# Gates of an adaLN block computed as columns, the last chunk's second half done block by block, and a new order of the stages

## The reference

```python
mod = (_silu(L0_c) @ L0_wmod).reshape(L0_c.shape[0], 6, 1, -1)
sa, ca, ga, sb, cb, gb = (mod[:, 0], mod[:, 1], mod[:, 2], mod[:, 3], mod[:, 4], mod[:, 5])
ga = (2 * (ga >= 0) - 1) * jnp.maximum(jnp.abs(ga), 0.25)
gb = (2 * (gb >= 0) - 1) * jnp.maximum(jnp.abs(gb), 0.25)
h = _layernorm(x, axis=-1) * (1 + ca) + sa
x = x + ga * attn(h)
h = _layernorm(x, axis=-1) * (1 + cb) + sb
x = x + gb * ffn(h)
```

## Time and profile before

| | |
|---|---|
| median of 3 runs | 470.56 us (470.47 to 470.79) |
| the profiled execution | 470.41 us |
| its span | 468.4 us |
| busy: PE, DVE, ACT, POOL | 420.9, 356.3, 302.0, 268.8 us |
| mean granted clock of PE | 0.984 |

### The profile page before, as it was taken

One profiled execution on the slowest core, in us unless ns is written; L12 is line 12 of the kernel. 1 busy time (PEld: TensorE's weight loads), 2 busy tenths in 40 slices (PEclk: granted clock), 3 DMA queues, 4 the chain that ended last, 5 costly groups with the idle time before them and its releaser, 6 DMA issues.

```text
span 468.4 us, 11145 instructions
## 1 busy us (share of the span) xinstructions
PE 420.9 (90%) x4170; PEld 270.2 (58%) x4170; DVE 356.3 (76%) x675; ACT 302.0 (64%) x974; POOL 268.8 (57%) x309
## 2 busy tenths in 40 slices
PE   3589949989989999999999999999897979888976
PEld 0265527666677656776667766666474744453432
DVE  4769989897978889878878786768867896646531
ACT  2445567987888798688568867666876866522210
POOL 4220726311775677756448776667528779976271
PEclk9799979999999999999999999999999999999999
DMA  8999763352474669536738836556842264672532
GB/s 318 235 397 388 207 206 46 59 123 47 80 147 113 158 133 202 143 84 115 181 72 157 163 49 145 111 139 117 156 115 46 47 136 90 153 142 45 136 80 77
DMA packets 144901, 65.09 MB, mean 139 GB/s; under 512 B 134704, under 2 KB 134960, under 8 KB 144464
## 3 DMA queue, kind: packets, MB, share of 16 engines
q1 hardware_dynamic: 144704, 64.37, 57.7%
q10 hardware_dynamic: 144, 0.02, 0.1%
HBM read 26.63 MB, written 4.19 MB: 66 GB/s over the span
## 4 chain that ended last, share of the span: by engine, by line
PE 51%; DVE 16%; POOL 10%; DMA 9%; ACT 6%; issue 5%; SPq 2%; ACTq 0%; POOLq 0%; DVEq 0%
PE F L1024 15%; PE C L1133 12%; PE C L1024 10%; PE W L1024 3%; PE S L1179 3%; PE W L1196 3%; ACT prob L705 3%; DMA xa<-in_x_dram 3%; POOL prob L584 2%; DVE p L915 2%; DMA gT<-g 2%; PE S L1024 2%; DMA xb<-in_x_dram 2%; DVE nm L909 2%; DVE qk L895 2%
## 5 line engine op out<-in xcount | busy, mean ns | idle before, releaser
L1133 PE MATMUL C<-hT,cw 128*128 128x256 f16 x864 | 108.4, 277 | 13.0 <-DVE cv L886 6.9
L584 POOL TENSOR_TENSOR prob<-prob,rinv 128x1024 f32<-128x1024 f32 x32 | 62.4, 1948 | 73.7 <-DVE rinv L920 73.7
L1133 PEld LDWEIGHTS C<-hT,cw 128*128 128x128 f16 x864 | 83.0, 99 | 32.1 <-issue 7.4
L705 ACT ACTIVATE prob<-S,nms 128x128 f32<-128x128 f32 x256 | 89.9, 377 | 7.1 <-DVE p L915 6.0
L1024 PE MATMUL F<-btw,gT 128*128 128x512 f16 x336 | 74.8, 379 | 2.2 <-DMA gT<-g 2.1
L676 ACT ACTIVATE qk<-C,bqk 128x256 f16<-128x256 f32 x128 | 52.6, 479 | 14.2 <-PE C L1024 13.4
L895 DVE SCALAR_TENSOR_TENSOR qk<-C,bqk,qk 128x256 f16<-128x256 f32 x128 | 54.3, 474 | 4.6 <-ACT qk L676 4.6
L1024 PEld LDWEIGHTS F<-btw,gT 128*128 128x128 f16 x336 | 32.5, 98 | 40.7 <-DMA gT<-g 2.9
L705 ACT ACTIVATION_READ_ACCUMULATOR prob<-S,nms 128x1 f32 x256 | 55.5, 217 | 0.0
L1024 PE MATMUL C<-cv,pw 128*128 128x256 f16 x384 | 50.4, 273 | 2.4 <-DVE cv L886 1.9
L915 DVE SCALAR_TENSOR_TENSOR p<-prob,p 128x1024 f16<-128x1024 f32 x32 | 48.3, 1509 | 4.6 <-ACT p L714 4.3
(11 more groups left out here) (187 smaller groups left out, 722.2 us busy)
## 6 DMA issues: line engine op xcount, KB each, us to landing
xa<-in_x_dram SPq DMA_DIRECT2D x10, 512.0 KB, 4.3
xb<-in_x_dram SPq DMA_DIRECT2D x6, 512.0 KB, 5.0
wmb<-in_wmod_dram SPq DMA_DIRECT2D x1, 3072.0 KB, 19.1
out_dram<-xb SPq DMA_DIRECT2D x12, 256.0 KB, 2.4
cw_raw<-in_cw_dram SPq DMA_DIRECT2D x3, 768.0 KB, 5.3
raw<-in_cw_dram SPq DMA_DIRECT2D x3, 768.0 KB, 5.2
wma<-in_wmod_dram SPq DMA_DIRECT2D x4, 512.0 KB, 6.9
bt_raw<-in_btw_dram SPq DMA_DIRECT2D x2, 1024.0 KB, 9.7
```

Source lines behind the costliest of these rows:

```text
L584: nc.gpsimd.tensor_tensor(prob[:], prob[:], rinv[:, i % 2].unsqueeze(2).broadcast_to([P, 8, P]), ALU.mult).then_inc(p_normal, 1)
L705: ins = nc.scalar.activation(prob[:, h], S[i % len(S)][h // 4][:, (h % 4) * P:(h % 4 + 1) * P], ACT.Exp, bias=nms[:, i % 2, h:h + 1], scal ...
L1133: ins = nc.tensor.matmul(bank_c[:, 0:CH], cw[:, i, a, c, tap, :], hT[:, j % 2, b, c, OWN - 1 + tap:OWN - 1 + tap + CH], start=step == 0, s ...
```

## The change

Four things are changed.

1. **Gates as columns.** row:0:2 makes one group of rows in place of two copies. A new stage cols:0:2 turns it into columns, cols:0:1 does so with gb as well, and `clamp` works on 128 x 8 values, in five operations (a copy comes first). Each pick is four products of 128 columns with a full identity in place of one of 512. The tile sel is now a view of that identity, so POOL makes two fewer constants.
2. **First stages by hand.** cols:0:0 comes before hs:1:0; hs:1 is two stages, a block each; all of the first 33 convolution products stand together; pj's last operation on DVE is a stage of its own, pk.
3. **Last chunk.** l2a, l2b, hs2, lr, ro and rw of chunk 7 are two stages each, a block each. The products lr:7:0 and lr:7:1 take a C bank each; POOL's six root operations run once for each block.
4. **A new order** of all stages.

```diff
-        na:0:0 sil:0:0 halo:0:0 nb:0:0 na:1:0 hs:0:0 row:0:0 nb:1:0 hs:1:0 cols:0:0 sp:0:0 c:0:6 sp:0:1 sp:0:2 c:0:9
...
+        na:0:0 sil:0:0 nb:0:0 na:1:0 hs:0:0 row:0:0 nb:1:0 cols:0:0 hs:1:0 sp:0:0 halo:0:0 halo:1:0 hs:1:1 c:0:33
...
+        ident = put("ident", [P, P], F32)
+        gate = put("gate", [P, 2, DC, NB], F32)
+        tmpcol = put("tmpcol", [P, 2, DC, NB], F32)
...
+        ffn_blocks = lambda j, n: (n,) if j == NCH - 1 else (0, 1)
+        ffn_cols = lambda j, n: slice(n, n + 1) if j == NCH - 1 else slice(0, 2)
...
+        h_blocks = lambda j, n: (n,) if j == 1 else (0, 1)
...
-                    for b in range(2):
+                    for b in h_blocks(j, n):
                         sp.wait_ge(h_lo, 2 * j + b + 1)
...
-                    if j < 2:
-                        sp.dma_start(cw_raw[:, j + 1], cw_in[:, j + 1]).then_inc(ld[f"cw{j + 1}"], 16)
-                    if j == 1:
+                    if j + n < 2:
+                        sp.dma_start(cw_raw[:, j + n + 1], cw_in[:, j + n + 1]).then_inc(ld[f"cw{j + n + 1}"], 16)
+                    if j == 1 and n == 1:
...
-            def clamp(rows, at, to):
-                g, a, b = rows[at:to, :], tmprow[at:to, 0], tmprow[at:to, 1]
+            def clamp(g, columns):
+
+                a, b = tmpcol[:, 0], tmpcol[:, 1]
+                link(nc.vector.tensor_copy(g, columns))
                 link(nc.vector.scalar_tensor_tensor(out=a, in0=g, scalar=-1.0, in1=g, op0=ALU.mult, op1=ALU.max))
                 link(nc.vector.tensor_scalar(b, g, 0.0, 2.0, ALU.is_ge, ALU.mult))
                 link(nc.vector.tensor_scalar(a, a, 0.25, None, ALU.max))
...
+                    if n > 0:
+                        ins = clamp(gate[:, 2 - n], at[:, rows - 1, :, 0:NB])
...
                     nc.vector.tensor_tensor(pjt[:], pjw_raw[:], gaB[:, n], ALU.mult).then_inc(pj_prod, 1)
+                elif s == "pk":
                     dve.wait_ge(pj_hi, n + 1)
...
-                        for i, m in enumerate([(0, 1), (), (2, 2), (0, 1, 2)][n]):
+                        for i, m in enumerate([(0, 1), (), (2,), (0, 1, 2)][n]):
...
+                        for k in range(DC):
+                            ins = nc.tensor.matmul(m_bank(stage)[:, k * P:(k + 1) * P],
+                                                   gate[:, n // 2, k, b:b + 1].broadcast_to([P, P]), ident[:],
+                                                   start=True, stop=True)
...
-                    for moved in h2_moved:
-                        pe.wait_ge(moved, 16 * (j + 1))
+                    for b in ffn_blocks(j, n):
+                        pe.wait_ge(h2_moved[b], 16 * (j + 1))
```

More of the change, by code:

```diff
@@ new lines, in bass_adaln_block @@
+        e:0:1 pj:0:1 cols:0:1 c:1:6 nz:0:1 c:1:21 bias:0:0 c:1:3 pk:0:1 c:1:6 v:0:3 v:0:0 s:0:2 c:1:3 m:0:2 ph:0:1
+        nb:3:0 qk:1:0 c:1:3 xr:0:0 sp:0:10 c:1:6 qk:1:1 e:0:2 c:1:12 nz:0:2 pick:0:2 c:1:3 pv:0:0 c:1:9 s:0:3 m:0:3
+        pick:0:3 ph:0:2 na:4:0 qk:1:4 pv:0:1 qk:1:5 c:1:9 e:0:3 c:1:3 nz:0:3 c:1:24 hs:3:0 fbias:0:0 qk:1:6 halo:3:0
+        v:1:3 v:1:1 s:1:0 m:1:0 ph:0:3 qk:1:3 sp:0:8 e:1:0 c:2:6 pick:0:4 c:2:6 nz:1:0 c:2:12 pv:0:2 qk:1:2 c:2:12
+        qk:1:7 s:1:1 m:1:1 ph:1:0 pv:0:3 qk:2:0 v:1:0 e:1:1 nb:4:0 c:2:3 xr:1:0 c:2:15 nz:1:1 c:2:18 v:1:2 qk:2:1
@@ L316, in bass_adaln_block @@
         split_first = lambda n: sum(len(SPLITS[i][0]) for i in range(len(SPLITS)) if SP_USE["sp", 0, i] < SP_USE["sp", 0, n])
[L318 removed]
+        by_c = lambda m, b: [modT[:, m // 2, c, b:b + 1] for c in range(DC)]
         def conv_split(n, src, b, loaded):
@@ L1223, in _ @@
                 elif s == "fb":
-                    for moved in h2_moved:
-                        pe.wait_ge(moved, 16 * (j + 1))
+                    pe.wait_ge(h2_moved[n], 16 * (j + 1))
                     use = 2 * j + n
```

221 lines of the change are left out of this document (103 added, 118 removed).

## The result

The changed kernel takes **468.18 us** (median of 13 runs), the kernel before 470.79 in the same runs: ratio 0.9934, 95% interval 0.991 to 0.9959. It is faster, and 468.18 lies in the range, but I had forecast 1.6% and 0.66% came. A second series of both gave 0.9924 (0.9897 to 0.9951).

What follows compares the result with a forecast made beforehand. PE, busy for 90% of the span, was taken as the bound. 470.41 - 3.0 (early part) - 3.3 (last chunk) - 1.0 (order between 400 and 420) = 463.1, stated as 463.2 us; range 457.5 to 469.

Steps and rivals of the forecast that it cites:

- Gates, DVE: Two gate clamps on DVE take 0.95 us each instead of 2.3 and 5.7; with pk apart, 7.5 us saved together.
- Gates, PE: Picks and extra transposes before 80 us add 2.0 us of PE work (1.5 to 3.7).
- The wait that is moved: Chunk 2's hT transposes land behind the bs_raw and bt_raw loads; PE waits 4.0 us (0 to 5) for the halo.
- Rival 1: On SP's queue transposes do not queue behind the loads, so the 4.0 us wait goes: 458.4 us, chance 0.16.
- Tail: Last chunk block by block shortens PE's waits for h (0.92) and gT (2.36): -3.3 us, other bound -0.9.
- The 6.9 us go whole: PE's single 6.9 us wait for DVE, ending at 67.27 us, vanishes because DVE reaches chunk 1's first evacuation earlier.
- the sum of the early part, -3.0: Early terms -6.9, +2.0, +4.0, -0.8 give -1.7; fewer PE waits on DVE between 70 and 140 us add -1.3.
- the 0.8 us of clock: Half of the 1.6 us lost to PE's halved clock after the 6.9 us wait returns: -0.8 us (0 to 1.6).
- Elsewhere the order changes but not the work, 0: Outside the early part, last chunk and 400 to 420 us, the new order costs 0 (-3 to +5).
- Rival 2: The new order adds some six small PE waits in the middle, +4.3 us: 467.5 us, chance 0.17.
- Rival 4: PE is held by the three C banks at chunk ends, 14.5 us lost: 477.7 us, slower, chance 0.06.
- Order between 400 and 420: Stages v:7:1, v:7:3 and pv:7:0 moved behind s:7:3 fill PE waits of 1.93 and 0.91: -1.0 us (0 to -2.8).

Runs made afterwards that it cites:

- loads apart: Changed kernel with the three 1 MB loads bs_raw and bt_raw (twice) issued singly behind the first three softmax-tile transposes on SP's queue: 0.9803 of the kernel before, 463.8 us.
- the split behind fb:3:0: Changed kernel with those loads issued singly and sp:0:14, the second batch's base-weight split, moved behind fb:3:0: 0.9762 of the kernel before, 461.16 us.
- the two runs that moved the loads: Changed kernel with bs_raw and bt_raw loads issued behind chunk 2's transposes and x load (1.0012, 473.09 us), or singly behind three softmax-tile transposes (0.9803, 463.8 us).

## Why the prediction was wrong, step by step

| what was changed | ratio | 95% interval | so, % |
|---|---|---|---|
| tail | 0.9912 | 0.9878 to 0.9947 | -0.9 |
| gates, old order | 1.0038 | 1.0008 to 1.0067 | +0.4 |
| all edits, old order | 0.9947 | 0.9921 to 0.9972 | -0.5 |
| all edits, new order (the changed kernel) | 0.9924 | 0.9897 to 0.9951 | -0.8 |
| the same, loads apart | 0.9803 | 0.9761 to 0.9844 | -2.0 |
| and the split behind fb:3:0 | 0.9762 | 0.9743 to 0.9781 | -2.4 |

**What was right.** *Gates, DVE:* a clamp takes 1.0 us in both places (forecast 0.95), five operations 0.2 apart:

```profile
42.60 0.16 DVE L783 COPY gate<-F 128x8 f32<-128x8 f32 x1
42.79 0.17 DVE L784 SCALAR_TENSOR_TENSOR tmpcol<-gate 128x8 f32<-128x8 f32 x1
...
43.40 0.17 DVE L787 SCALAR_TENSOR_TENSOR gate<-tmpcol 128x8 f32<-128x8 f32 x1
```

*Gates, PE:* forecast 2.0 us of added work. The rows give about 1.3: the new transposes take 0.43 us, the picks 2 and 3 1.06 and 1.16 in place of 1.12 each, and the picks 0 and 1 1.95 (forecast 2.4) in place of 1.13. (PE's busy time grew by 2.3 us over the run, but that holds the low clock too. And the forecast's upper bound is low by its own rate: 0.45 us for each product makes 4.3, not 3.7.)

```profile
44.49 1.95 PE L1109 MATMUL S<-ident,gate 128*128 128x128 f32 x16
```

*First stages*, taken at nothing: the first convolution product starts at 17.29 us (before 19.73), but PE then waits 2.2 us for cw_raw and 1.7 for cv, and row 3 starts at 49.57, before at 49.53. *The wait that is moved:* forecast 4.0 us for a halo copy, ending near 64, with hT landing over 8 us after issue; measured 5.2, ending at 65.95, 8.6 (the last load landed near 64 and not at 62.7). *Rival 1*, that the transposes do not queue, fell by that, and its price was about right from the other side: I had put 4.8 us between it and the forecast, and the loads apart brought 1.2%, 5.7 us. *Tail:* forecast 3.3 us, 4.1 (2.5 to 5.8) alone.

**Step "The 6.9 us go whole": failed.** I took what DVE saves, 7.5 us, and compared it with the wait. But DVE's chain to cv starts behind row 3's product, and with the gates alone PE brings that 2.2 us later: DVE's evacuation of cv starts at 64.32 us in place of 66.74, 2.4 us earlier and not 7.5. Behind it the next waits are for prob, which ACT makes after a transpose has landed, and they grew. Alone, the saving took 1.9 us of the 6.9, and the gates were a loss. With the new order and the loads apart they pay 0.7%. In the changed kernel the halo wait covers this: the sum of the early part, -3.0, looks right (idle time -5.9 in 60 to 150 us, busy time +2.3), but 3.4 of these 5.9 lie between 105 and 150 us, where all edits in the old order still waited as before (3.1). They are the order's, not the gates'. And the 0.8 us of clock did not come back: after 5.2 us of waiting it was 0.50 again from 66 to 70 us. Nor is a pause of 4.0 us the edge that I took it for, since it also fell behind the 2.0 us waits of the two runs that moved the loads.

**Step "Elsewhere the order changes but not the work, 0": failed.** My reason was that the work stays the same, which says nothing of the waits. The 0 hid the two largest terms, of opposite sign: +7.7 us in 150 to 330 and -6.0 in 330 to 400, +1.7 together. I had looked at how far a score stage stands ahead of its pv and not at stages that wait for the end of another (sp:0:14), which alone held 0.6%. Rival 2, small waits in the middle, +4.3, was the nearest of the four (467.5 for 468.18); I gave it 0.17 and no place. That its time fits so well is partly luck: the waits cost 7.7, and the -6.0 stood in no rival. Rival 4's waits, for a C bank that is not yet emptied, can be only the small ones there (1.3 for xb, 0.4 for cv); 3.5 for att and 2.2 for gT are others.

**Step "Order between 400 and 420", -1.0: failed**, +1.2 between 400 and 425. The first wait for gT there is 1.8 after 1.93, the 0.91 is 0.91 again, and one of 1.10 for DVE's ob stands there that was not. Whether the doubt I noted, two evacuations ahead of the softmax on DVE, is the cause, the rows don't show and no run tried; this part stays open.

**Tail in the changed kernel:** 37.3 us from fl:5:1 to the end of the products (before 39.64), a gain of 2.3 and not 3.3. The wait of 0.92 for h, which I had let go, is still there: lr:7:0 is so short (0.6 us) that the second block's transpose is needed 1.5 us after the first:

```profile
440.16 0.59 PE L1030 MATMUL C<-arw,h 128*128 128x80 f16 x12
441.67 0.60 PE L1030 MATMUL C<-arw,h 128*128 128x80 f16 x12 [0.92 <-DMA h<-h]
```

The forecast was 463.1 for the profiled execution, and 469.3 came, 6.2 more. By the table of idle times: 150 to 400 us +1.7, 400 to 425 +2.2, the tail +1.0, and 60 to 150 us -1.7 (the halo wait 1.2 longer than forecast, other waits 2.9 shorter). PE's busy time grew by 2.3 where +2.0 of work and -0.8 of clock were forecast, so +1.1. That is 4.3; some 2.0 more are idle time before 60 us, which the second profile of the changed kernel does not have.

## What to carry to other kernels

Before moving a transpose on a queue, list every large load that will then stand ahead of it, and place each load by itself behind a transpose and ahead of its first reader: here that was worth 1.2%, more than the whole change had brought. An engine's saved time is not the wait that ends on it; ask what else is in that chain. And a new order is not free where PE was full: look for the stages that wait for the end of another stage, and for how the idle time is shared out over the run, before writing 0.

## What the runs showed of the hardware

- Transposes issued right behind 3 MB of loads landed late: hT 7.4 to 9.8 us after issue and pt 11.3; with the loads apart hT took 3.2 to 4.6 and pt 4.2 to 5.3. While hT waited, from 56 to 60 us, the core moved 418 to 422 GB/s. The Trainium skill's page "DMA: Bandwidth & Descriptors" (queues, rings and completion order) says that each DMA engine consumes descriptors in ring order; the traces agree: the last load landed near 64 us, and hT, issued behind it, at 65.5.
- The clock's answer to a wait is not fixed: after a 2.0 us wait for cv at 66.7 it fell to 0.50 in the profile with the loads apart and stayed at 1.00 in that with the split moved too, with the same waits from 35 us up to there. Late in the run it differs too: behind a gT wait of 1.99 us near 407 with the gates alone it was 0.57 in 408 to 412, and the group of gT products took 7.04 us; before, behind 1.93 us, it was 1.00 and the group took 5.35.
- The products of row 2 took 3.63 us over two groups of output rows before and take 3.62 over one in the changed kernel: here dropping a group freed nothing, as the forecast had it.
